# Six-layer fp32 block on one core: queries as three rounded products begun in the fp4 layer, an earlier correction load, the last two layers merged tile by tile

## The reference, cut to what matters

```python
x = x + L0_xattn(ln(x), ctx)        # local attention with rotary positions
x = x + L0_attn(ln(x))              # self-attention over the 64 positions of a batch
x = x + L0_ffn(ln(x))               # gate/up/down product on fp4-rounded values
x = x + L1_xattn(ln(x), ctx)        # cross attention, 16 heads, relative tables, 1601 keys
x = x + L1_attn(ln(x))              # time mix (a scan), then channel mix:
#   kk = square(relu(xk2 @ Wk.T));  kv = kk @ Wv.T;  x + sigmoid(xr2 @ Wr.T) * kv
x = x + L1_ffn(ln(x))               # KAN: s = x @ Win + bin
#   h = relu(s[..., None] * W1 + b1);  g = sum_h(h * W2) + b2;  out = g @ Wout + bout
```

## Time and profile before

| | us |
|---|---|
| three runs | 1509.21, 1509.92, 1511.82 (median 1509.92) |
| the profiled execution, its own time | 1511.36 |
| its span, first to last instruction | 1509.3 |
| PE busy in it | 1416.2 |
| DVE, ACT, POOL busy | 728.9, 509.0, 368.4 |
| mean granted clock of PE | 0.960 of full |

### The profile page before, as it was taken

How to read it: one execution, slowest core, us unless ns; L and a number is a source line. 1 busy time by engine, 2 the same in 40 slices (tenths; PEclk the granted TensorE clock), 3 DMA queues, 4 the chain that set the end, 5 groups by cost and what they waited for, 6 DMA issues and landing times. The chain is left out here.

```text
span 1509.3 us, 26710 instructions
## 1 busy us (share of the span) xinstructions
PE 1416.2 (94%) x11200; PEld 1058.5 (70%) x11200; DVE 728.9 (48%) x1337; ACT 509.0 (34%) x839; POOL 368.4 (24%) x228
## 2 busy tenths in 40 slices
PE   7889987899998999999999999999999997997995
PEld 6858774545457788888887887887878865434783
DVE  6669779789463323322323233223232233676933
ACT  3434222333121153433432534234325343613702
POOL 7120100000131331312231313132313111306911
PEclk9779979999989999999999999999999999999997
DMA  5412200102034121111110211111102016003000
GB/s 205 168 57 77 78 1 1 77 0 84 0 111 128 52 64 33 52 38 58 40 55 28 64 33 52 38 57 41 56 26 64 23 53 257 1 0 133 0 1 28
DMA packets 49573, 88.01 MB, mean 58 GB/s; under 512 B 28584, under 2 KB 41136, under 8 KB 46128
## 3 DMA queue, kind: packets, MB, share of 16 engines
q1 hardware_dynamic: 49456, 86.32, 16.5%
HBM read 76.61 MB, written 9.70 MB: 57 GB/s over the span
## 5 line engine op out<-in xcount | busy, mean ns | idle before, releaser
L1345 POOL TENSOR_TENSOR ctx_hi<-ctx_raw,one 128x1536 fp32r<-128x1536 f32 (+1 forms) x32 | 91.5, 2858 | 567.4 <-DMA ctx_raw<-in_ctx 363.9
L1543 ACT COPY ET<-PS 128x512 f32<-128x512 f32 (+1 forms) x224 | 129.4, 585 | 276.8 <-PE PS L1447 201.4
L1646 DVE TENSOR_SCALAR_CACHE_REDUCE E<-PS 128x384 f32<-128x384 f32 (+1 forms) x256 | 131.8, 571 | 180.6 <-PE PS L1424 180.0
L1615 DVE TENSOR_TENSOR V<-PS,vbias 128x512 f32<-128x512 f32 (+1 forms) x104 | 71.7, 690 | 192.9 <-PE PS L1391 192.8
L1391 PE MATMUL PS<-ctx_raw_r,wk_hi 128*128 128x384 f32 (+1 forms) x512 | 128.2, 355 | 0.0
L1391 PE MATMUL PS<-wv_lo,ctx_hi 128*128 128x512 f32 (+1 forms) x416 | 127.6, 406 | 0.0
L1550 ACT ACTIVATE E<-E,peak 128x1601 f32<-128x1601 f32 x64 | 103.5, 1622 | 66.9 <-DVE peak L1651 66.9
L1447 PE MATMUL PS<-ident,E 128*128 128x128 f32 (+1 forms) x832 | 122.9, 273 | 0.0
L1391 PE MATMUL PS<-ctx_hi,wk_hi 128*128 128x384 f32 (+1 forms) x512 | 120.6, 357 | 1.5 <-POOL ctx_raw_r L1348 1.5
L1391 PE MATMUL PS<-wv_hi,ctx_hi 128*128 128x512 f32 (+1 forms) x416 | 120.4, 411 | 0.8 <-issue 0.8
L1348 POOL TENSOR_TENSOR ctx_raw_r<-ctx_raw,ctx_hi 128x1536 fp32r<-128x1536 f32 (+1 forms) x32 | 116.9, 3653 | 2.5
(11 more groups left out here) (320 smaller groups left out, 2225.4 us busy)
## 6 DMA issues: line engine op xcount, KB each, us to landing
ctx_raw<-in_ctx SPq DMA_DIRECT2D x24, 768.0 KB, 4.4
ctx_raw<-in_ctx_first SPq DMA_DIRECT2D x8, 900.0 KB, 4.5
rel_scr<-rel_out SPq DMA_DIRECT2D x8, 640.0 KB, 3.6
fwk<-in_fwk SPq DMA_DIRECT2D x1, 4096.0 KB, 12.4
fwv<-in_fwv SPq DMA_DIRECT2D x1, 4096.0 KB, 12.4
corr<-rel_scr SPq DMA_DIRECT2D x64, 48.0 KB
p_scr<-E SPq DMA_DIRECT2D x16, 192.0 KB, 2.3
near<-p_scr SPq DMA_DIRECT2D x64, 48.0 KB
```

Of the source, the lines that this page charges most:

```text
L1345: nc.gpsimd.tensor_tensor(ctx_hi[r][:, :, 0:n], ctx_raw[r][:, :, 0:n], one[:].unsqueeze(1).broadcast_to([P, KC, n]), ALU.mult).then_inc(S[ ...
L1543: nc.scalar.copy(ET[0:n, j % ET_RING, :], src[0:n, :]).then_inc(S["et_out"], 1)
L1615: v.tensor_tensor(V[0:rows, at % V_RING, :], bank(4 + NUMBER[unit] % 2)[0:rows, :], vbias[0:rows, :], ALU.add).then_inc(S["v_out"], 1)
L1646: v.tensor_scalar(E[:, p, k0:k0 + n], bank(r)[:, 0:n], 1.0, None, ALU.mult, ALU.max, accum_out=tops[:, p, c:c + 1]).then_inc(S["s_out"], 1)
```

## The change

What it does, in four parts.

1. The turns of XN for the queries, the rounded parts of the query weights (ACT), their rests (DVE), the rounded parts and rests of the turned tiles (ACT, DVE), and the split of the value weights (DVE) move into the end of the fp4 layer's block. The queries are `split_product`s: 48 matmuls of rounded parts for 16 plain float32 ones.
2. The first correction is loaded behind the seventh store of relative products (of eight), ahead of the eighth.
3. The second channel product waits for the hidden groups one by one instead of for all.
4. The KAN layer has no block any more. Its work is done in the channel mix's block by token tile: turns, input products and output products of a tile stand inside the second channel product of later tiles.

The diff, cut to its core:

```diff
 def fp4_layer(...)
+            after.apply(dve, 0, s.X, s.XN)
+            for c in range(KC):
+                dve.wait_ge(q_hi, c + 1)
+                nc.vector.tensor_tensor(s.wq_lo[:, c], s.wq[:, c], s.wq_hi[:, c].bitcast(F32), ALU.subtract).then_inc(q_lo, 1)
+            residual(2)
+            after.apply(dve, 1, s.X, s.XN)
+            dve.wait_ge(s.l_wkv, 32)
+            dve.wait_ge(turned, len(groups))
+            nc.vector.tensor_copy(s.wv_hi[:], s.raw_wv[:]).then_inc(v_hi, 1)
+            after.apply(dve, 2, s.X, s.XN)
+            dve.wait_ge(v_hi, 1)
+            nc.vector.tensor_tensor(s.wv_lo[:], s.raw_wv[:], s.wv_hi[:].bitcast(F32), ALU.subtract).then_inc(v_lo, 1)
+            residual(3)
+            after.apply(dve, 3, s.X, s.XN)
+            for t in range(NT):
+                dve.wait_ge(xt_hi, t + 1)
+                nc.vector.tensor_tensor(s.xt_lo[...t], bank(t)..., s.xt_hi[...t].bitcast(F32), ALU.subtract).then_inc(xt_lo, 1)
 scalar
+            act.wait_ge(s.l_wq, 16)
+            for c in range(KC):
+                nc.scalar.copy(s.wq_hi[:, c], s.wq[:, c]).then_inc(q_hi, 1)
+            for t in range(NT):
+                act.wait_ge(after.transposed, t + 1)
+                nc.scalar.copy(s.xt_hi[...t], bank(t)...).then_inc(xt_hi, 1)
 tensor
+            for t in range(NT):
+                after.tensor(pe, t, bank(t), s.XN, s.ident[:])
 def cross_attention(...)  sync
             for b in range(B):
                 ...
                 sp.dma_start(rel_scr[b]...).then_inc(rel_stored[b % 2], 16)
-            load_corr(sp, 0)
+                if b == B - 2:
+                    load_corr(sp, 0)
 tensor
-            for t in range(NT):
-                nm.tensor(pe, t, bank(t), s.XN, s.ident[:])
-            pe.wait_ge(nm.xt_ready, NT)
-            pe.wait_ge(l_wq, 16)
             for g in range(KC):
-                linear_to_features(nc, bank(4 + g), wq, g, s.XT).then_inc(S["q_ps"], 1)
+                split_product(nc, bank(4 + g), ((wq_hi, wq_lo), (xt_hi, xt_lo))).then_inc(S["q_ps"], 1)
 scalar, vector
-            nm.scalar(act, t, bank(t), s.XT)                  # four turned tiles
-            v.tensor_copy(wv_hi[:], raw_v[:]) ...; v.tensor_tensor(wv_lo[:], ...)
 def channel_mix(...)  tensor
             pe.wait_ge(S["v_split"], 2 * HC)
-            pe.wait_ge(S["h_hi"], HC)
+            pe.wait_ge(S["gate_in"], NT)
+            pe.wait_ge(s.loaded["kan"], 64)
             for t in range(NT):
                 k = 0
+                pe.wait_ge(S["relu"], HC - 3 + t)
                 for x, w in (...three pairs...):
-                    if k == 2 * HC:
-                        pe.wait_ge(S["h_lo"], HC)
                     for g in range(HC):
+                        if t == 0 and k < HC:
+                            pe.wait_ge(S["h_hi"], g + 1)
+                        if t == 0 and k >= 2 * HC:
+                            pe.wait_ge(S["h_lo"], g + 1)
+                        if t >= 2 and k == 4:
+                            outputs(t - 2)
+                        if t in (1, 2) and k == 20:
+                            turn(t - 1)
+                        if t in (1, 2) and k == 28:
+                            inputs(t - 1)
                         last = nc.tensor.matmul(...)
+            turn(2), inputs(2), turn(3), inputs(3), outputs(2), outputs(3)
 scalar
+            for t in range(NT):
+                after.scalar(act, t, bank(t), s.XT)
+                act.wait_ge(S["u_ps"], t + 1)
+                nc.scalar.activation(unit[tile t], bank(t)[:, 0:P], ACT.Identity, bias=...).then_inc(S["unit"], 1)
+                act.wait_ge(S["unit"], t + 1)
+                if t >= 2:
+                    act.wait_ge(S["acc"], HALF * (t - 1))
+                for i in range(HALF):
+                    nc.scalar.activation(inner[:, t % 2, i, :], unit[tile t], ACT.Relu, bias=b1[i], scale=w1[i]).then_inc(S["inner"], 1)
 gpsimd, for each t
                 after.pool(pool, t)
+                pool.wait_ge(after.tile_ready, t + 1)
+                nc.gpsimd.tensor_tensor(s.X[:, t, :], s.X[:, t, :], bout[:], ALU.add).then_inc(S["biased"], 1)
 vector   (inner_sum: one tensor_scalar and seven scalar_tensor_tensor of 128x128, each waiting for the one before)
+            residual(0), inner_sum(0), residual(1), add_output(0), inner_sum(1), residual(2), add_output(1), residual(3)
+            inner_sum(2), inner_sum(3), add_output(2), add_output(3)
-def kan_layer(...)            # the whole block is removed; SP stores a tile after its add_output
```

More of the change, by code:

```diff
@@ L875, in fp4_layer @@
     s.l_wq, s.l_wkv = sem("l_wq1"), sem("l_wkv1")
+    s.wq_lo = b6.rounded("wq")
+    values = Region(nc, s.after_base)
+    s.wv_hi, s.wv_lo = values.tensor("wv_hi", [P, KC, D], F32R), values.tensor("wv_lo", [P, KC, D], F32R)
+    s.wv_end = values.at
+    s.q_parts_at = s.zone + 4096
+    parts = Region(nc, s.q_parts_at)
+    s.wq_hi, s.xt_hi = parts.tensor("wq_hi", [P, KC, D], F32R), parts.tensor("xt3_hi", [P, KC, TOK], F32R)
+    s.q_parts_end = parts.at
+    assert s.q_parts_end <= s.zone + 4 * KC * INNER
+    q_hi, q_lo, v_hi, v_lo, xt_hi, xt_lo = (sem("b5_" + n) for n in ("q_hi", "q_lo", "v_hi", "v_lo", "xt_hi", "xt_lo"))
     wg, wu = s.w["wg"], s.w["wu"]
@@ L2015, in _ @@
                 sp.dma_start(t[:], src).then_inc(s.loaded["kan"], 16)
+            for t in range(NT):
+                sp.wait_ge(S["out_done"], t + 1)
+                sp.dma_start(s.out[:, t, :], s.X[:, t, :]).then_inc(S["stored"], 16)
+            sp.wait_ge(S["stored"], 16 * NT)
         @block.gpsimd
@@ L2102, in _ @@
             square(HC - 1)
+            act.wait_ge(s.loaded["kan"], 64)
+            for t in range(NT):
+                after.scalar(act, t, bank(t), s.XT)
+                act.wait_ge(S["u_ps"], t + 1)
+                nc.scalar.activation(unit[:, t * P:(t + 1) * P], bank(t)[:, 0:P], ACT.Identity,
+                                     bias=kan[:, 3 * HALF:3 * HALF + 1]).then_inc(S["unit"], 1)
+                act.wait_ge(S["unit"], t + 1)
+                if t >= 2:
+                    act.wait_ge(S["acc"], HALF * (t - 1))
+                for i in range(HALF):
+                    nc.scalar.activation(inner[:, t % 2, i, :], unit[:, t * P:(t + 1) * P], ACT.Relu, bias=b1[:, i:i + 1],
+                                         scale=w1[:, i:i + 1]).then_inc(S["inner"], 1)
         @block.vector
@@ L2131, in _, with residual @@
                 rest_of_hidden(g)
-            for t in range(NT):
+            def residual(t):
                 out = flat(y[:])[:, t]
@@ new lines, in inner_sum @@
+            def inner_sum(t):
+                part = acc[:, t * P:(t + 1) * P]
+                for i in range(HALF):
+                    dve.wait_ge(S["inner"], HALF * t + i + 1)
+                    if i == 0:
+                        v.tensor_scalar(part, inner[:, t % 2, 0, :], w2[:, 0:1], kan[:, 3 * HALF + 1:3 * HALF + 2],
+                                        ALU.mult, ALU.add).then_inc(S["acc"], 1)
+                    else:
+                        dve.wait_ge(S["acc"], HALF * t + i)
+                        v.scalar_tensor_tensor(part, inner[:, t % 2, i, :], w2[:, i:i + 1], part, ALU.mult, ALU.add).then_inc(S["acc"], 1)
@@ L2268, in perceiver_kernel @@
         channel_mix(nc, step, s, n6, n7)
-        kan_layer(nc, step, s, n7)
 def by_chunk(a):
```

113 lines of the change are left out of this document (37 added, 76 removed).

## The result

The changed kernel takes 1496.83 us (four runs: 1494.33, 1494.46, 1499.19, 1499.74) where the kernel before took 1510.26 in the same session; ratio 0.9908, 95% interval 0.9894 to 0.9923. Run again later: 1494.93 (1493.75 to 1497.77) against 1508.89, ratio 0.9905 [0.9889, 0.9922]. The profiled execution took 1494.33 us; its span is 1492.4, granted clock 0.966 (before: 1511.36, 1509.3, 0.960).

A forecast was written before the change was run, and what follows sets the result against it. PE was taken as the bound, busy 1416.2 of 1509.3 us. Queries and correction 5.1 plus second product and KAN 11.1 gave 16.2 us: span 1493.1, execution 1495.2, at the runs' median 1493.7; range 1490.0 to 1500.5.

The forecast's parts named there:

- likeliest case: Whole kernel: the forecast itself, 16.2 us won and 1493.7 us, given chance 0.55.
- Block start and relk_ready: Cross attention's start: block begins 2.6 us later, DVE's memset at 438.25, PE waits 1.8 to 4.2 us before relative(0).
- Queries win 2.1: Cross attention's start: relative(1) at 442.6 against 444.70, so the queries win 2.1 us, not 4.4 to 6.9.
- The first rival: Before relative(0): PE's wait for relk_ready costs the clock, 2.3 us of gain lost, 1496.0 us; chance 0.18.
- the case that the prediction named against this rival: Before relative(0): clock already fallen between 413 and 419, so queries end later and the gap is 1.8 us.
- First correction, "5.1 earlier for both": Period 0 of the cross attention: queries and correction order together bring PE 5.1 us earlier, bounds 2.1 and 5.9.
- the rival "the order does nothing": First correction: its DMAs land when they landed before, relative to the store; 3.0 us less, 1496.7 us; chance 0.12.
- the context load goes at 472.8: SP's queue, behind the corrections and eighth store: the context load is issued at 472.8, 5.1 us earlier.
- Second product by group, 2.5: Between the channel products: PE's wait of 2.33 us goes, 2.5 us won with the issue gap; bounds 0 and 2.5.
- KAN by tile: Kernel's tail: last store ends at 1498.2 instead of 1509.3; with the second product by group, 11.1 us won.
- The rival "small instructions cost like large": KAN tail: links cost 0.85 us each, end at 1503.4 for 1498.2, so 1498.9 us; chance 0.08.
- Slower: Period 0 of the cross attention: PE's clock falls and does not come back, up to 1513.7 us; chance 0.02.

The follow-up runs named there:

- a_filler: The changed kernel plus three unused 512-column matmuls on PE ahead of its wait for relk_ready before relative(0): 1497.20 us, ratio 0.9916.
- a_split: The changed kernel with three corrections behind the seventh store, then the eighth store, third context chunk and other five corrections: 1497.79 us, ratio 0.9923.
- q_only: The kernel before with part 1 of the change alone: 1509.97 us, ratio 1.0002.
- kan_both: The kernel before with parts 3 and 4 of the change alone: 1498.18 us, ratio 0.9922.
- group_only: The kernel before with part 3 of the change alone: 1507.33 us, ratio 0.9982.
- a_no_order: The changed kernel without part 2, the first correction back behind the eighth store: 1499.21 us, ratio 0.9923.
- a_tables: The changed kernel with relative key table and key bias loaded first, on their own semaphore, and prepared first by DVE: 1494.84 us, ratio 0.9900.
- a_rests: a_tables with DVE's four rests of the key weights moved behind its copies of relative products 2 and 3: 1497.82 us, ratio 0.9923.

## Why the prediction was right, and where it was not

Predicted 1493.7 us, measured 1496.83 and 1494.93; likeliest case, though with parts of two rivals in it. 13.4 to 14.0 us were won for 16.2.

- **Block start and relk_ready: right.** Tied to residual(3), the block starts 2.19 us later (5.83 for 3.64) where I had 2.6, and the memset 2.45 later. PE idles before relative(0) with DVE's memset as the last releaser, 2.66 us, inside 1.8 to 4.2. That the queries' own 4.4 to 6.9 us would not come through was the step that mattered, and it held.
- **Queries win 2.1: too high by 0.9.** The first rival's mechanism took place, and with it one of the signs named for being wrong, half clock behind 438 (four products 1.91 us for 1.09): 1.36 us (5.26 for 3.90, `a_filler`), not 2.3. 1.2 are left at relative(1). Where the clock held, the same queries won 2.7 (relative(1) 28.96 us from residual(3) in `a_split`, 29.00 in `a_filler`, 31.65 before), a little more than forecast; `a_split` is the case that the prediction named against this rival, queries slowed first and then a short gap (1.65 us, where it had 1.8). So both cases are real. The four profiles with a gap of 2.5 to 2.8 us there lost the clock (5.26 or 5.27 us from relative(0) to relative(1)), the one with 1.65 kept it (3.80); I gave that rival 0.18, which was too low. The length of a gap alone does not decide: behind waits of 2.6 us at the scores 16 records took 1.48 us in `q_only` and 1.01 in `kan_both`, and 1.01 behind the 2.74 of the earlier trace rows. Timed alone the part lies between 1.5 us lost and 1.1 won.
- **First correction, "5.1 earlier for both": wrong by 2.3.** 2.78 us are won at the K unit in this pair of profiles (2.36 in the second profile); the order alone won 1.5 there, where the sum had 3.0, so the rival "the order does nothing" is half true. The step "the context load goes at 472.8" looks right (472.89), but all of it began 1.54 us early: measured from residual(3) the load is 3.48 us earlier (61.38 for 64.86), not 5.1. Of the 1.6 missing, 0.9 is what the queries fell short by and 0.7 the eighth store, which took SP 1.05 us behind the skewed loads instead of 0.36. Another 0.70 went at the landing: 479.30 - 472.89 = 6.41 us after the issue, where it was 483.62 - 477.91 = 5.71. So POOL's wait is 1.93 and not 1.2. The store, not the correction, released DVE (1.54 us), so PE kept 0.71 of the 2.74.
- **Second product by group, 2.5: right**: no gap, and from the channel mix's first product after its turns to this one 2.39 us less in the changed kernel and 2.50 in `group_only` and `kan_both`; 2.7 timed.
- **KAN by tile: right, nearly step by step.** From DVE's start on the last product tile: XN(3) after 3.91 us (3.9), relus of tile 3 start after 8.89 (9.1), its chain ends after 12.95 (12.7), the end after 17.6 (18.3). A relu of 128 columns took 3.18 / 8 = 0.40 us as worked out from the earlier trace rows, a link 3.08 / 7 = 0.44 for 0.45. The product took 48.77 us with all that was put into it, for 48.86. The rival "small instructions cost like large" is excluded, and with it the reading of "VectorE: DVE Perf Modes" (the Trainium skill, section on the TRN2 errata) that speaks against small tiles; its fixed cost per instruction is there (a link costs 0.44 for 128 columns, 0.84 for 512), but the count of links on the path decides. What was off: outputs(3) ran near full clock (1.13 us for two records, one of the bounds); in the profile of `a_no_order` the same two records took 2.07, and the end came 0.96 us later. 9.42 us won by the marks.
- **Slower: not seen**; the clock was back to 1.00 from 442 on.

The sum of the profiles: 2.78 for parts 1 and 2, 2.39 and 9.42 for 3 and 4, 0.97 - 0.20 between, 1.54 ahead: 16.9, the difference of the spans. That my 16.2 comes close to it is in part luck: 1.54 no edit earned, and of the 0.77 between none is known; the runs' own medians differ by 13.4 to 14.0. The errors of my sum are both in waits that follow a removed wait.

## What to carry to other kernels

Before pricing faster products, list what they wait for behind them: here three waits stood in a row (small tables, rests of the weights, corrections), and taking one only moved it to the next, until all were moved but one. Take DVE's small preparations out from beside large GpSimd instructions: order their loads first, and give them a semaphore of their own (0.37 us for 6.46 here, though alone it did not make the kernel faster). A layer that is one chain through five engines is best cut by tile into the dense products ahead of it; price its last tile by lengths of small instructions from the trace.

## What the runs showed of the hardware that I had not expected

- DVE beside GpSimd: four additions of one column 6.46 us and 0.37 alone; 128x159 3.57 and 0.32; four of 128x512 7.91 and 2.50. The rule of the Trainium skill cited in the prediction ("SBUF — State Buffer", section "SBUF: two separate sides") is borne out by `a_tables`, and in the changed kernel by where the groups end: the four additions at 432.20 and the 128x159 at 436.30, GpSimd's instructions beside them at 432.12 and 436.12. The ratio is worst for the smallest.
- The same program took from 1493.75 to 1499.74 us, and the profiles of all kernels show the granted clock differ in the same few stretches. At 80 to 100 us, work that no kernel changes, it was between 1.00 and 0.74; over the last 20 us of the cross attention it was 1.00 or 0.91, and from the K unit to that layer's end it took 782.2 to 783.0 us at the one and 783.8 to 785.3 at the other (twelve profiles; two more, of `a_filler` and `a_rests`, had lost clock right behind the K unit and took longer); at the last output products 1.13 or 2.07 us for the same two records. A gain under 3 us has to be read from a distance between two marks with as few such stretches in it as can be, and even then one profile can mislead (1.25 us in `group_only`).
- A store of 0.36 us on SP took 1.05 to 1.28 us when it stood behind skewed loads.
